# A two-layer decoder on one core: where three sets of f16 halves are made — the retention's weights, the context and the rotation generator's weights

## The reference, cut to what matters

```python
# softmax attention: q over its features, k and v over the tokens
q = softmax(h @ Wq.T + bq, -1); k = softmax(h @ Wk.T + bk, -2) / 16; v = softmax(h @ Wv.T + bv, -2)
x += (q @ k.T) @ v                                      # h = ln(x)
# retention, 16 heads of 16; keys and values from the context
q, k, v = rot(ln(x) @ W_Q), rot(ctx @ W_K), ctx @ W_V   # rot: position tables cos, sin
ret = normed_per_head((q @ k.T) * decay @ v)
x += ret * silu(ln(x) @ g_w.T + g_b) @ out_w.T + out_b
# experts: the best 2 of 8 for each token
x += sum_e w_e * ((sigmoid(u) * u * (ln(x) @ W2[e])) @ W3[e])   # u = ln(x) @ W1[e]
# rotation by a generator
params = ln(x).mean(tokens) @ omega_proj_w.T + omega_proj_b     # 2016 numbers for each sample
G = I + O + O@O/2 + O@O@O/6                                     # O antisymmetric 64x64 from params
x += rmsnorm(h + omega_mix*(h[:, :, :64] @ G @ omega_out_w.T + b) + vq_mix*vq(mean))  # h = ln(x)
x += attention(ln(x), one key and value head from ctx)
x += shared_and_routed_silu_experts(ln(x))
```

## Time and profile before

| what | value |
|---|---|
| median of 3 runs | 1692.19 us (1686.76 to 1697.7) |
| the profiled execution | 1696.84 us, its span 1695.0 us |
| start of the retention | 179.9 us |

### The profile page before, as it was taken

The page is one execution under the profiler, slowest core; times in us unless marked ns, Lnnn a source line. Parts: engine busy times, 40 slices in busy tenths (PEclk is TensorE's granted clock), DMA queues, the critical chain, the costliest instruction groups (busy, mean ns, idle before and its releaser), DMA issues. The chain is left out here.

```text
span 1695.0 us, 33484 instructions
## 1 busy us (share of the span) xinstructions
PE 1288.7 (76%) x12367; PEld 975.7 (58%) x12367; DVE 1043.2 (62%) x2043; ACT 810.9 (48%) x1528; POOL 684.5 (40%) x615
## 2 busy tenths in 40 slices
PE   5888468787774359999999636882778784699997
PEld 2555246666653348888888536732456562356654
DVE  5987457777665465555555394554688863576654
ACT  4666245666542323333333244131367677466653
POOL 1110269999862024444444223051287786000000
PEclk9999688887865569999999855556788885799999
DMA  5553767646605302222122270007542420230330
GB/s 223 184 188 113 187 130 125 108 89 112 88 3 235 165 26 64 64 60 63 59 63 61 64 292 1 2 1 144 122 77 58 77 34 1 101 113 27 113 126 26
DMA packets 102121, 160.53 MB, mean 95 GB/s; under 512 B 14150, under 2 KB 70730, under 8 KB 100428
## 3 DMA queue, kind: packets, MB, share of 16 engines
q1 hardware_dynamic: 92940, 133.47, 30.1%
q0 software_dynamic: 8640, 24.65, 4.6%
q10 hardware_dynamic: 384, 0.26, 0.1%
HBM read 102.21 MB, written 48.10 MB: 89 GB/s over the span
## 5 line engine op out<-in xcount | busy, mean ns | idle before, releaser
L2752 POOL TENSOR_TENSOR q_pl<-q_ex,q_ph 128x512 f16<-128x512 f32 x128 | 147.1, 1160 | 43.9 <-ACT q_ph L2713 43.3
L1699 POOL TENSOR_TENSOR r_siml<-r_sim,r_simh 128x512 f16<-128x512 f32 x128 | 146.0, 1159 | 18.3 <-ACT r_simh L1601 18.0
L997 POOL DMA_INDIRECT expert_results<-mt_yout,m_deliver x78 | 77.4, 993 | 172.2 <-ACT mt_yout L1085 160.1
L2568 DVE TENSOR_REDUCE q_mx<-q_pS 128x4 f32<-128x512 f32 x128 | 86.6, 685 | 68.6 <-PE q_pS L2496 68.0
L1458 DVE TENSOR_TENSOR r_sim<-r_pS,r_causal 128x512 f32<-128x512 f32 x128 | 86.6, 682 | 57.1 <-PE r_pS L1372 53.3
L1601 ACT ACTIVATE r_simh<-r_sim 128x512 f16<-128x512 f32 x128 | 80.0, 628 | 87.0 <-DVE r_sim L1458 82.8
L1030 PE MATMUL mt_pU<-mt_xh,m_w 128*128 128x256 f16 x624 | 116.2, 274 | 1.5 <-DVE mt_xl L1106 1.5
L1030 PE MATMUL mt_pV<-mt_xh,m_w 128*128 128x256 f16 x624 | 115.4, 273 | 0.0
L1041 PE MATMUL mt_pY<-m_w,mt_hh 128*128 x624 | 106.6, 272 | 10.9 <-DVE mt_hl L1120 10.8
L1079 ACT ACTIVATE mt_hh<-ahead 128x512 f16<-128x512 f32 x78 | 49.1, 630 | 126.6 <-DVE ahead L1115 125.1
L2964 PE MATMUL s_pY<-s_w,s_hh 128*128 128x256 f16 x576 | 101.1, 275 | 8.0 <-DVE s_hl L3186 6.6
(11 more groups left out here) (516 smaller groups left out, 4023.5 us busy)
## 6 DMA issues: line engine op xcount, KB each, us to landing
s_spread_share<-shares SPq DMA_DIRECT2D x32, 512.0 KB, 6.7
a_pf<-in_L_ffn_W SPq DMA_DIRECT2D x24, 512.0 KB, 6.2
m_w<-split_w SPq DMA_DIRECT2D x6, 2048.0 KB, 22.1
split_w<-a_ph SPq DMA_DIRECT2D x24, 256.0 KB, 3.6
split_w<-a_pl SPq DMA_DIRECT2D x24, 256.0 KB, 3.8
r_kstack<-k_bounce SPq DMA_DIRECT2D x48, 128.0 KB, 4.7
...
```

The lines of the kernel that those rows point to most:

```text
L997: pool.indirect_dma_start(results[:, :], bass.IndirectOffsetOnAxis(ap=deliver[:, at:at + 1], axis=0), yout[n % 2][:, a, :], None).then_inc ...
L1699: pool.tensor_tensor(siml[n % RING][:, :], sim[n % SIMS][:, :], simh[n % RING][:, :], ALU.subtract)\
L2568: dve.tensor_reduce(mx[:, at:at + UNIT], pS[n % 2][:, :, :], AX, ALU.max).then_inc(s["taken"], 1)
L2752: pool.tensor_tensor(pl[n % RING][:, :], ex[n % 3][:, :], ph[n % RING][:, :], ALU.subtract)\
```

## The change

Three sets of halves are made at other places.

- The retention's five weights are split in the softmax stage, from `ahead` into tiles that now live from there to the end of the retention: the centring on DVE in step 3 of the loop, a high half on ACT in each of steps 3 to 7 (`later_upper`), a low half on DVE in each of steps 4 to 8 (`later_lower`). Their order becomes Q, K, g, o, V.
- The context's halves are made in the softmax stage, one group a step: SP loads `a_ctx`, ACT makes the high half (`context_high`, behind the three `piece_upper`), POOL the low half (`context_lower`, behind `norm_v`), SP stores both to `ctx_parts`. The retention loads halves from there: two DMAs of 512 KB a group in place of one load of 1 MB and two stores. Behind the start of its steps its load waits for V's projection two groups back. The bias row's operation on DVE moves behind the first row statistics (step -41).
- The generator's weights are split in the expert tiles, in eight pieces of 1024 columns: from tile 3 on, every fourth tile a high half on ACT behind the tile's step, and a low half on DVE one tile later; SP loads and stores. Their halves lie in DRAM (`omega_parts`), and the rotation stage loads them with two DMAs behind its results and constants, with nothing left there for ACT, POOL and DVE to do on them.

```diff
@@ -155,9 +155,12 @@
...
+                def load_context(g):
+                    sp.dma_start(cf[g % 2][:, :].rearrange("p (a n) -> p a n", a=DC), A["ctxT"][:, :, g * GT:(g + 1) * GT])\
+                      .then_inc(ctx_in[g % 2], 16)
+
+                def store_context(g):
+                    sp.wait_ge(ctx_low, g + 1)
+                    for t in range(2):
+                        sp.dma_start(A["ctx_parts"][t, g], ctx16[t][g % 2][:, :]).then_inc(ctx_out[g % 2], 16)
...
+                    store_context(n)
+                    if n + 2 < NG:
+                        load_context(n + 2)
...
+                def centre_v():
+                    dve.wait_ge(later_in, 16 * len(RETENTION))
+                    dve.tensor_reduce(wsum[:, :], by_head, AX, ALU.add).then_inc(v_summed, 1)
+                    dve.wait_ge(v_summed, 1)
+                    dve.scalar_tensor_tensor(by_head, spread(wsum[:, :], HD), -1.0 / HD, by_head, ALU.mult, ALU.add)\
+                       .then_inc(v_centred, 1)
...
+                def later_lower(i):
+                    n = RETENTION[i]
+                    dve.wait_ge(later_high, i + 1)
+                    dve.scalar_tensor_tensor(flat(R[n][1]), later[n], HALVES_SCALE, flat(R[n][0]), ALU.mult, ALU.subtract)\
+                       .then_inc(later_low, 1)
...
+                    if j == 3:
+                        centre_v()
+                    if 0 <= j - 4 < len(RETENTION):
+                        later_lower(j - 4)
...
+                def context_high(g):
+                    act.wait_ge(ctx_in[g % 2], 16 * (g // 2 + 1))
+                    if g >= 2:
+                        act.wait_ge(ctx_out[g % 2], 32 * (g // 2))
+                    act.activation(ctx16[0][g % 2][:, :], cf[g % 2][:, :], ACT.Copy).then_inc(ctx_high, 1)
...
+                def later_upper(i):
...
+                    act.wait_ge(later_in, 16 * len(RETENTION))
+                    if n == "V":
+                        act.wait_ge(v_centred, 1)
+                    act.activation(flat(R[n][0]), later[n], ACT.Copy, scale=HALVES_SCALE).then_inc(later_high, 1)
...
+                    on(j, piece_upper(0), piece_upper(1), piece_upper(2), context_high)
+                    if 0 <= j - 3 < len(RETENTION):
+                        later_upper(j - 3)
...
+                def context_lower(g):
+                    pool.wait_ge(ctx_high, g + 1)
+                    pool.tensor_tensor(ctx16[1][g % 2][:, :], cf[g % 2][:, :], ctx16[0][g % 2][:, :], ALU.subtract)\
+                        .then_inc(ctx_low, 1)
...
-                    on(j - 1, norm_v)
+                    on(j - 1, norm_v, context_lower)
...
+    def piece_due(n):
+        i, rest = divmod(n - FIRST_PIECE, TILES_PER_PIECE)
+        return i if rest == 0 and 0 <= i < len(pieces) else None
...
+                if n >= PIECES_IN_FLIGHT:
+                    m = n - PIECES_IN_FLIGHT
+                    sp.wait_ge(piece_low, m + 1)
+                    for t, half in enumerate((ph, pl)):
+                        sp.dma_start(omega_parts[t][:, pieces[m]], half[m % PIECES_IN_FLIGHT][:, :])\
+                          .then_inc(piece_out[m % PIECES_IN_FLIGHT], 16)
+                if n < len(pieces):
+                    sp.dma_start(pf[n % PIECES_IN_FLIGHT][:, :], omega[:, pieces[n]])\
+                      .then_inc(piece_in[n % PIECES_IN_FLIGHT], 16)
...
+                act.activation(ph[i][:, :], pf[i][:, :], ACT.Copy, scale=OMEGA_SCALE).then_inc(piece_high, 1)
...
+                if piece_due(n) is not None:
+                    piece_upper(piece_due(n))
...
+                dve.wait_ge(piece_high, n + 1)
+                dve.scalar_tensor_tensor(pl[i][:, :], pf[i][:, :], OMEGA_SCALE, ph[i][:, :], ALU.mult, ALU.subtract)\
...
+                if piece_due(n - 1) is not None:
+                    piece_lower(piece_due(n - 1))
...
-                    if g > 0:
-                        sp.wait_ge(s["ctx_l"], g)
-                    sp.dma_start(cf[:, :, :], A["ctxT"][:, :, g * GT:(g + 1) * GT]).then_inc(s["ctx_in"], 16)
...
-                def keep_context(g):
-                    sp.wait_ge(s["ctx_h"], g + 1)
-                    sp.wait_ge(s["ctx_l"], g + 1)
+                    if g >= 2:
+                        sp.wait_ge(s["v_projected"], DC * (g - 1))
                     for t, half in enumerate((ch, cl)):
-                        sp.dma_start(A["ctx_parts"][t, g], flat(half[g % 2][:])).then_inc(ctx_kept[g % 2], 16)
+                        sp.dma_start(flat(half[g % 2][:]), A["ctx_parts"][t, g]).then_inc(ctx_in[g % 2], 16)
...
-                sp.wait_ge(s["weights_low"], len(names))
...
-                    g = due(t, -33)
-                    if g is not None:
-                        keep_context(g)
...
-                        pe.wait_ge(s["weights_low"], 2)
-                        pe.wait_ge(s["ctx_l"], g + 1)
+                        pe.wait_ge(ctx_in[g % 2], 32 * (g // 2 + 1))
...
+                    if t == -41:
+                        dve.wait_ge(s["bias_high"], 2)
+                        dve.scalar_tensor_tensor(rows[ONES:ONES + 1, :], bias[ONES:ONES + 1, :], SCALE, bias16[ONES:ONES + 1, :],
+                                                 ALU.mult, ALU.subtract).then_inc(s["bias_low"], 1)
 
...
-                dve.wait_ge(weights_in, 16 * len(names))
-                dve.tensor_reduce(wsum[:, :], held["V"].rearrange("p (h e) -> p h e", e=HD), AX, ALU.add)\
...
-                dve.scalar_tensor_tensor(held["V"].rearrange("p (h e) -> p h e", e=HD), spread(wsum[:, :], HD), -1.0 / HD,
...
-                for i, n in enumerate(names):
-                    dve.wait_ge(s["weights_high"], i + 1)
-                    dve.scalar_tensor_tensor(flat(W[n][1]), held[n], SCALE, flat(W[n][0]), ALU.mult, ALU.subtract)\
-                       .then_inc(s["weights_low"], 1)
...
-                    act.wait_ge(s["ctx_in"], 16 * (g + 1))
-                    if g >= 2:
-                        act.wait_ge(s["v_projected"], DC * (g - 1))
-                        act.wait_ge(ctx_kept[g % 2], 32 * (g // 2))
-                    act.activation(ch[g % 2][:, :, :], cf[:, :, :], ACT.Copy).then_inc(s["ctx_h"], 1)
...
-                    g = due(t, -40)
-                    if g is not None:
-                        context_high(g)
...
-                for n in names:
-                    if n == "V":
-                        act.wait_ge(s["v_centred"], 1)
-                    act.activation(flat(W[n][0]), held[n], ACT.Copy, scale=SCALE).then_inc(s["weights_high"], 1)
...
-                    pool.wait_ge(s["ctx_h"], g + 1)
-                    if g >= 2:
-                        pool.wait_ge(ctx_kept[g % 2], 32 * (g // 2))
-                    pool.tensor_tensor(cl[g % 2][:, :, :], cf[:, :, :], ch[g % 2][:, :, :], ALU.subtract)\
-                        .then_inc(s["ctx_l"], 1)
...
-                    g = due(t, -38)
-                    if g is not None:
-                        context_low(g)
...
-                    if g in (1, 3, 4, 5):
-                        columns = each(piece * WIDE, WIDE)
-                        sp.dma_start(Wp[:, columns], flat(A["L1_attn_Wp"])[:, columns]).then_inc(s["wp_in"], 16)
-                        piece += 1
...
+                for t in range(2):
+                    sp.dma_start(flat(Wp16[t][:]), A["omega_parts"][t]).then_inc(s["wp_in"], 16)
...
-                sp.wait_ge(s["wp_low"], 4)
...
-                    columns = each(n * WIDE, WIDE)
-                    act.wait_ge(s["wp_in"], 16 * 4)
-                    act.activation(Wp[:, columns], Wp[:, columns], ACT.Copy, scale=PSCALE).then_inc(s["wp_scaled"], 1)
-                    act.wait_ge(s["wp_scaled"], n + 1)
-                    act.activation(flat(Wp16[0][:])[:, columns], Wp[:, columns], ACT.Copy).then_inc(s["wp_high"], 1)
...
-                    pool.wait_ge(s["wp_high"], n + 1)
-                    pool.tensor_tensor(flat(Wp16[1][:])[:, columns], Wp[:, columns], flat(Wp16[0][:])[:, columns],
```

93 lines of the change are left out of this document (48 added, 45 removed).

## The result

The changed kernel takes 1680.08 us, the median of 8 runs (1675.89 to 1683.65), against 1694.46 us for the kernel before in 8 runs (1686.76 to 1697.70). The ratio is 0.9932, with a 95% interval from 0.9906 to 0.9957: faster by 7 to 16 us, and within the 1% that the prediction called no change. The forecast was 1672.3 with a range from 1663 to 1686; the number of the second case, "the retention does not follow", was 1680.7.

The account below looks back on a forecast made before the run. No engine fills the span and stages have different limits: DVE paces softmax, POOL limits most of a steady retention group. Terms 4.1 + 3.8 - 7.4 - 8.5 + 0.3 - 12.2 = -19.9 us, from 1692.19 to 1672.3; range 1663 to 1686.

Parts of the forecast that it names:

- the second case: Retention: the steady part gives only 3 us and the start 4.5, total 1680.7 us; chance 0.32.
- Rotation stage, -12.2 us: Rotation stage: slow DVE adds return to usual time and ACT's last `l_XN` starts earlier; -12.2 us, bounds -11 and -13.
- the fourth rival: Rotation stage: PE's clock rises to 2.4 GHz for the generator's matmuls, total 1661 us; chance 0.05.
- Start of the retention, -7.4 us: Start of retention: PE begins K of group 1 at 209.0 instead of 216.44; -7.4 us, bounds -8.9 and -4.5.
- the 4 us that were named as a sign of being wrong: Start of retention: K of group 1 waiting for its context by more than 4 us would make the prediction wrong.
- Steady retention, -8.5 us: Retention groups 3 to 7: POOL, taken as the limit, loses 2.13 us a group, 1.7 credited each; -8.5 us.
- Softmax, +7.9 us: Softmax loop: added DVE work costs +4.1 us and DVE waiting for POOL's context operation +3.8 us.
- POOL's meeting with `a_nqshift`: Softmax steps 2 to 7: DVE's `a_nqshift` waits 0.63 us for POOL's context low half to end; +3.8 us.
- the additions on DVE: Softmax: centring 1.3 us and four lower weight halves at 0.69 us, all uncovered on DVE's chain; +4.1 us.
- Expert tiles, +0.3 us: Expert tiles: eight ACT and eight DVE split operations nearly fit existing holes; +0.3 us, up to 3.
- the third: Softmax: ACT stalls on its context load and the kernel ends slower, 1711 us at 5.5 us a step; chance 0.05.
- the 0.35 for the middle: Whole kernel: chance 0.35 that the time counts as the same, within about 1% (17 us) of before.

Follow-up runs that it names:

- e2: The kernel before plus only the generator's part of the change (weights split in the expert tiles): 1681.54 us, ratio 0.9942 to the kernel before.
- e1: The kernel before plus only the softmax and retention part (retention weights and context halves): 1695.08 us, ratio 1.0010 to the kernel before.
- e9: The changed kernel itself, unedited, run again on a third chip: 1678.65 us, ratio 0.9916 to the kernel before.
- e5: The changed kernel plus an unused POOL operation per retention group at step -38, ahead of the rotated q: 1675.23 us, kernel before 1676.70 on that chip.
- e6: The changed kernel plus an unused POOL operation per retention group at step -31, behind the rotated k: 1688.24 us, kernel before 1676.70 on that chip.
- e7: The changed kernel with one retention score unit's low half on DVE instead of POOL: 1675.11 us, kernel before 1676.70 on that chip.
- e10: The changed kernel with DVE's centring and lower weight halves moved behind the softmax statistics' combination: 1676.55 us, ratio 0.9913 to the kernel before.
- e11: The changed kernel with DVE's weight operations behind the statistics' combination, second context loaded before zero fills, one score unit's low half on DVE: 1679.24 us, ratio 0.9915.

## Why the prediction was right, and where it was not

- **Rotation stage, -12.2 us.** Right, in its mechanism and to the digit: 177.04 to 164.83 us, and e2 shows that it is this part that the total gained. The working was that the additions fall back to their usual time and ACT, with nothing left in front of it, follows `l_shift` at once. Both are in the rows. The clock of this stage did not rise: in the windows of the changed kernel from 1033 to 1055 us, with PE busy in all but 0.15 of 22 us, it is 0.50, so the fourth rival falls.
- **Start of the retention, -7.4 us.** -5.4 in the changed kernel's trace, and the mean of seven traces with this start (66.98, 65.77, 66.04, 65.98, 64.60, 65.11 and 64.97) is 65.6, which is -6.7. The context of the second group waited behind the zero fills, as the working had it: 30.4 us after the stage's start, forecast 29.1. PE's wait for it, 3.92 us, stayed just below the 4 us that were named as a sign of being wrong.
- **Steady retention, -8.5 us.** This is the step that failed. It was worth nothing: 166.7 us before, 166.4 (e1, e9) and 168.1 with the change. "So POOL is the limit for most of a group" was read from a mean over whole groups, and a relief was credited without asking where in the group it is. e5 and e6 show the place: 2.1 us on POOL at step -38 cost at most 0.5, at step -31 they cost 1.9; and e7 shows that even in that stretch 0.65 us less did not make a group shorter. This was the second case (0.32), and with this term at 0 the forecast's own sum gives 11.4 us, against 14.4 between the medians and 11.5 by the ratio. That the second case's 1680.7 lies so near the measured 1680.08 is in part luck: it had 3 us for the steady groups and 4.5 for the start, and the traces have 0 and 5.4 to 6.7.
- **Softmax, +7.9 us.** Near in number, but by another sum, which is luck. The eight traces with this code have 135.5 us on the mean, the two with the old one 127.7. Against e2, whose clock did not fall in these steps, the changed kernel's intervals from one `a_nqmax` to the next grew by 0, 0.63, 4.59, 2.07, 0.61, 0.62 and 0, 8.5 us in all. POOL's meeting with `a_nqshift` came three times at 0.62, 1.9 and not 3.8 (afterwards the slow projection had moved DVE away from it); the additions on DVE show as 1.3 and twice 0.6, 2.5 and not 4.1, since in the last steps the longer hole at `a_nqmax` (2.58 and 3.67 us) takes them in. What I had not priced at all is PE: 2.65 us in step 3 and 1.5 in step 4. DVE's work between PE's last product and the addition to `X` lengthened PE's gap (1.59 us in e2, 3.08 and 2.19 here), and PE came back at half its clock. With that work elsewhere the gap was 1.76 us and step 3 took 19.3 us in e10 and e11, not 22.8; but a short gap was no guarantee, as the last section counts.
- **Expert tiles, +0.3 us.** Nothing speaks against it: 0.1 between e1 and e2, one trace each.
- **The rivals.** ACT never waited for a load in the softmax (0.35 us ahead of `a_aT`, forecast 0.1 to 0.7), so the third did not come. The chance for faster by over 1% was 0.60, and it is the 0.35 for the middle that came true, on the one term whose doubt had been named beside it ("POOL is idle 2.7 us a group already").
